# A fused Macaron block on one core: the third norm's rows turned by memory and VectorE instead of TensorE

## The reference, cut to what matters

```python
x = L0_attn_x                                   # (4, 1024, 1024) float32
x = x + 0.5 * ffn(layernorm(x))                 # first norm
x = x + attn(layernorm(x))                      # second norm
x = x + 0.5 * ffn(layernorm(x))                 # third norm

def ffn(input):      # same weights both times
    x = input.reshape(-1, 1024)
    hits = softmax(x @ centroids.T / 0.1) > 0.01          # 64 clusters
    query_sel = any(hits, axis=1)                         # per token
    row_sel = any(hits, axis=0)[assignments]              # per output column
    return where(query_sel[:, None] & row_sel[None, :], x @ weight.T + bias, 0)

def attn(x):         # per token: 32 heads as a 32 x 32 softmax over the head dimension
    q, k, v = x @ Wq + bq, x @ Wk + bk, x @ Wv + bv       # k and v: 8 heads, each repeated 4 times
    scores = einsum('bsdh,bseh->bsde', q, k) / sqrt(32)
    return einsum('bsde,bseh->bsdh', softmax(scores), v)
```

## Time and profile before

| | us |
|---|---|
| median of 3 runs | 1257.59 |
| lowest, highest | 1253.80, 1264.04 |
| profiled execution: span from first to last instruction | 1253.4 |
| TensorE busy | 1224.9 |
| VectorE busy | 841.3 |
| ScalarE busy | 411.3 |
| GpSimd busy | 419.6 |

### The profile page before, as it was taken

The page is one execution under the profiler, slowest core; times in us unless marked ns, Lnnn a source line. Parts: engine busy times, 40 slices in busy tenths (PEclk is TensorE's granted clock), DMA queues, the critical chain, the costliest instruction groups (busy, mean ns, idle before and its releaser), DMA issues.

```text
span 1253.4 us, 21699 instructions
## 1 busy us (share of the span) xinstructions
PE 1224.9 (98%) x8552; PEld 1052.8 (84%) x8552; DVE 841.3 (67%) x1207; ACT 411.3 (33%) x590; POOL 419.6 (33%) x551
## 2 busy tenths in 40 slices
PE   6999999999998899999999999999999999999998
PEld 5778888888887788888888888888888888887886
DVE  5644355345452378878788787887878865279887
ACT  4313222322210134443444444444444443212120
POOL 1225544543423634323333333333332200040322
PEclk8999999999998999999999999999999999999999
DMA  7376776776663345555555555455555554116785
GB/s 260 101 210 184 231 199 201 198 223 176 168 179 117 110 124 155 156 135 163 156 139 157 141 158 162 133 160 139 152 160 133 148 142 162 67 51 236 275 302 193
DMA packets 318693, 208.53 MB, mean 166 GB/s; under 512 B 258304, under 2 KB 281344, under 8 KB 318592
## 3 DMA queue, kind: packets, MB, share of 16 engines
q1 hardware_dynamic: 303712, 187.74, 52.0%
q10 hardware_dynamic: 14880, 19.40, 4.5%
HBM read 118.49 MB, written 88.60 MB: 165 GB/s over the span
## 4 chain that ended last, share of the span: by engine, by line
PE 90%; DVE 3%; DMA 2%; ACT 1%; issue 1%; SPq 1%; POOL 1%; POOLq 0%; DVEq 0%; ACTq 0%
PE ps_b L269 13%; PE ps_b L271 13%; PE ps_b L270 13%; PE ps_a L269 11%; PE ps_a L271 10%; PE ps_a L270 10%; PE ps_t L276 6%; PE ps_s L1348 5%; PE ps_s L283 2%; PE ps_s L285 2%; PE ps_s L1398 2%; PE ps_s L290 1%; DMA y_scratch<-xa 1%; SPq L398 1%; DMA ya_tok<-y_scratch 1%
## 5 line engine op out<-in xcount | busy, mean ns | idle before, releaser
L269 PE MATMUL ps_a<-w_hi,odd_hi 128*128 128x512 f32 x464 | 186.4, 402 | 0.0
L271 PE MATMUL ps_a<-w_hi,odd_lo 128*128 128x512 f32 x464 | 182.1, 392 | 0.0
L270 PE MATMUL ps_a<-w_lo,odd_hi 128*128 128x512 f32 x464 | 181.6, 391 | 0.0
L269 PE MATMUL ps_b<-proj_hi,y_hi 128*128 128x256 f32 (+1 forms) x512 | 177.7, 347 | 0.0
L271 PE MATMUL ps_b<-proj_hi,y_lo 128*128 128x256 f32 (+1 forms) x512 | 172.7, 337 | 0.0
L270 PE MATMUL ps_b<-proj_lo,y_hi 128*128 128x256 f32 (+1 forms) x512 | 172.0, 336 | 0.0
L303 POOL TENSOR_TENSOR var_eps<-moments,eps 128x1 f32<-128x1 f32 x96 | 18.4, 191 | 406.2 <-DVE moments L299 406.2
L661 POOL TENSOR_TENSOR x_ring<-x_ring,f_tmp 128x1024 f32<-128x1024 f32 x32 | 77.0, 2405 | 163.6 <-DVE probs L1112 135.4
L962 DVE TENSOR_TENSOR f_out<-ps_b,bias_a 128x512 f32<-128x512 f32 x30 | 20.7, 689 | 147.9 <-PE ps_b L271 147.9
L607 POOL TENSOR_SCALAR f_out<-f_out,token_on 128x1024 f32<-128x1024 f32 x30 | 85.6, 2854 | 88.3 <-DVE f_out L962 88.0
L271 PEld LDWEIGHTS ps_b<-proj_hi,y_lo 128*128 128x128 f32 x512 | 97.1, 190 | 10.8
(11 more groups left out here) (188 smaller groups left out, 2731.5 us busy)
## 6 DMA issues: line engine op xcount, KB each, us to landing
xa<-in_L_attn_x SPq DMA_DIRECT2D x32, 512.0 KB, 5.2
f_tmp<-f_scratch SPq DMA_DIRECT2D x32, 512.0 KB, 4.4
x_ring<-in_L_attn_x SPq DMA_DIRECT2D x32, 512.0 KB, 3.3
f_scratch<-f_out SPq DMA_DIRECT2D x30, 512.0 KB, 4.0
x_scratch<-x_ring SPq DMA_DIRECT2D x30, 512.0 KB, 3.3
y_scratch<-xa SPq DMA_DIRECT2D x28, 512.0 KB, 3.7
ya_tok<-y_scratch SPq DMA_DIRECT2D x112, 128.0 KB, 3.2
late<-x_scratch SPq DMA_DIRECT2D x22, 512.0 KB, 6.9
```

Source lines behind the costliest of these rows:

```text
L269: pe.matmul(acc, hi[:, k, :], w_h[:, k, cols], start=(k == 0), stop=False)
L270: pe.matmul(acc, hi[:, k, :], w_l[:, k, cols], start=False, stop=False)
L271: last = pe.matmul(acc, lo[:, k, :], w_h[:, k, cols], start=False, stop=(k == KB - 1))
```

## The change

The third norm's tiles 0 to 29 are no longer turned by TensorE. ScalarE writes the norm into a buffer of its own (`y3_tok`) in an order of blocks; SP stores it to memory (`y3_d`) and loads it back (`y3_turn`) with the 32-row blocks side by side; VectorE transposes the 32 x 32 blocks; ScalarE copies the high part from SBUF, writing every fourth column, and **Pool** subtracts for the low part. The kept tiles 1 and 3 and the late tiles 5 to 29 are loaded from `y3_d` again, so that their norms are not computed twice. Tiles 30 and 31 stay with TensorE (`transpose_end`, `high_end`, `low_end`).

To make room for the round trip the order changes: `high_third` and the low part come one iteration after the norm, third products go from `i-5` to `i-6` with two of them in the last iteration, and pair logits and pair softmax go one iteration back.

```diff
+    y3_d = nc.dram_tensor("y3_scratch", (NT - 2, T4, P, EMB // T4), F32, kind="Internal").ap()
+            y3_tok, y3_turn = sb2("y3_tok", [P, EMB]), sb2("y3_turn", [P, EMB])
-        late_y = [probs, f_tmp]
+        late_y = [y3_turn, y3_tok, probs, f_tmp]
+        def turned(tile):
+            return tile[:, :].rearrange("p (b k i) -> p b k i", b=T4, k=KB)
+        def by_block(tile):
+            return tile.rearrange("p k (i b) -> p b k i", b=T4)
 # SP
+                def store_y3(t):
+                    sp.wait_ge(y3, t + 1)
+                    sp.dma_start(y3_d[t].rearrange("a p f -> p a f"), y3_tok[:, :]).then_inc(y3_stored, 16)
+                def load_y3(t):
+                    sp.wait_ge(y3_stored, 16 * (t + 1))
+                    wait(sp, lo3, t)
+                    sp.dma_start(y3_turn[:, :], y3_d[t].rearrange(TURNED, b=T4)).then_inc(y3_in, 16)
+                def load_again(e):
+                    ...
+                    wait(sp, loe, e)
+                    sp.dma_start(f_tmp[:, :], y3_d[2 * e + 1].rearrange(TURNED, b=T4)).then_inc(ye_in, 16)
+                def load_late_y(v):
+                    ...
+                    wait(sp, lol, v - 4)
+                    sp.dma_start(late_y[n][:, :], y3_d[LATE[v]].rearrange(TURNED, b=T4)).then_inc(yl_in[n], 16)
                     if 3 <= i < NT + 1:
                         load_x(i + 1)
+                    if 0 <= i - 4 < NT - 2:
+                        store_y3(i - 4)
 ...                     # behind the q, k loads and the v store of iteration i
+                    if 0 <= i - 4 < NT - 2:
+                        load_y3(i - 4)
 # Pool
+                def low_third(t):
+                    hi, lo = third_set(t)
+                    pool.wait_ge(hi3, t + 1)
+                    pool.tensor_tensor(by_block(lo), turned(y3_turn),
+                                       by_block(hi.bitcast(F32)), ALU.subtract).then_inc(lo3, 1)
                     if i + 1 < NT:
                         mask_first(i + 1)
+                    if 0 <= i - 5 < NT - 2:
+                        low_third(i - 5)
+                    if i - 1 >= NT:
+                        low_again(i - 1 - NT)
+                    if i + 1 < NT:
                         add_first(i + 1)
+                for v in range(1, NL):
+                    for k in READY_OF[v - 1]:
+                        mask_ready(k)
+                    if 3 <= v + 1 < NL:
+                        low_late(v + 1)
 # ScalarE
+                def norm_third(t):
+                    act.wait_ge(norm3, t + 1)
+                    wait(act, y3_stored, 16 * t)
+                    normed(act, y3_tok[:, :].rearrange("p (a k j) -> p k a j", a=T4, k=KB), ...
+                def high_third(t):
+                    act.wait_ge(turn3, t + 1)
+                    ...
+                        if t % 2 == 0:
+                            act.wait_ge(ffn3, t)
+                    act.copy(by_block(third_set(t)[0]), turned(y3_turn)
+                             ).then_inc(hi3, 1)
+                    if 0 <= i - 6 < len(HALVES):
+                        store_third(i - 6)
                     if i == NT + 2:
-                        norm_third(NT - 2, i)
-                    if 0 <= i - 5 < len(HALVES):
                         store_third(i - 5)
+                        norm_end(NT - 2)
                     if 0 <= i - 4 < NT - 2:
-                        norm_third(i - 4, i)
+                        norm_third(i - 4)
+                    if 0 <= i - 5 < NT - 2:
+                        high_third(i - 5)
 # VectorE
+                def turn_third(t):
+                    dve.wait_ge(y3_in, 16 * (t + 1))
+                    dve.transpose(y3_turn[:, :], y3_turn[:, :]).then_inc(turn3, 1)
+                    if 0 <= i - 5 < NT - 2:      # ahead of row_max
+                        turn_third(i - 5)
-                    if 0 <= i - 4 < NT - 1:      # ahead of the transpose of probs
-                        low_third(i - 4)
 # TensorE
-                    if 0 <= i - 5 < len(HALVES):
+                    if 0 <= i - 6 < len(HALVES):
+                        product_third(i - 6)
+                    if i == NT + 2:
                         product_third(i - 5)
-                    if 0 <= i - 4 < NT - 1:
-                        transpose_third(i - 4, i)
-                    if NT <= i < NT + 2:
-                        transpose_again(i - NT)
-                    if v + 1 < NL:
-                        transpose_late(v + 1)
```

More of the change, by code:

```diff
@@ L186, in half, with wait_third @@
             return slice(h * HALF, (h + 1) * HALF)
+        def wait_third(eng, t):
+            if t < NT - 2:
+                eng.wait_ge(lo3, t + 1)
+            else:
+                eng.wait_ge(lo3_end, t - NT + 3)
         def wait(eng, semaphore, value):
@@ L561, in _ @@
                 sp.wait_ge(y3, NT - 2)
+                for v in range(1, 5):
+                    load_late_y(v)
                 load_late(4)
@@ L662, in add_first, with low_again, low_late @@
                                        ALU.add).then_inc(x1, 1)
+                def low_third(t):
[3 more added lines that the diff above has]
+                                       by_block(hi.bitcast(F32)), ALU.subtract).then_inc(lo3, 1)
+                def low_again(e):
+                    pool.wait_ge(hie, e + 1)
+                    pool.tensor_tensor(by_block(y2_lo[:, :, :]), turned(f_tmp), by_block(y2_hi[:, :, :].bitcast(F32)),
+                                       ALU.subtract).then_inc(loe, 1)
+                def low_late(v):
+                    hi, lo = late_set(v)
+                    pool.wait_ge(hil, v)
+                    pool.tensor_tensor(by_block(lo), turned(late_y[(v - 1) % 4]), by_block(hi.bitcast(F32)),
+                                       ALU.subtract).then_inc(lol, 1)
                 mask_first(0)
@@ L790, in high_again @@
                     act.wait_ge(te, e + 1)
[L791 to L797, removed]
+                    if e == 0:
+                        act.wait_ge(proj_v, NT)
+                    else:
+                        act.wait_ge(ffnk, 2)
+                    act.copy(by_block(y2_hi[:, :, :]), turned(f_tmp)).then_inc(hie, 1)
                 def keep_third(m):
@@ L829, in high_late @@
                 def high_late(v):
                     act.wait_ge(tl, v)
-                    act.copy(late_set(v)[0], ps_t[:, :, :]).then_inc(hil, 1)
-                def norm_third(t, i):
-                    act.wait_ge(norm3, t + 1)
-                    act.wait_ge(t2, min(i, NT))
-                    act.wait_ge(scores, min(i - 1, NT))
-                    wait(act, t3, t)
+                    if v == 1:
+                        act.wait_ge(ffnk, len(KEPT_HALVES))
+                        act.wait_ge(pair_done, 2 * NP)
@@ new lines, in high_third @@
+                def high_third(t):
+                    act.wait_ge(turn3, t + 1)
+                    if t < 2:
+                        act.wait_ge(pair_done, NP)
+                        for h in range(2):
+                            act.wait_ge(ffn1[h], NT - 1 + t)
+                    else:
+                        act.wait_ge(pair_done, NP + t // 2)
+                        if t % 2 == 0:
+                            act.wait_ge(ffn3, t)
+                    act.copy(by_block(third_set(t)[0]), turned(y3_turn)
+                             ).then_inc(hi3, 1)
@@ L838, in norm_third, with norm_end, high_end @@
+                def norm_end(t):
+                    act.wait_ge(norm3, t + 1)
+                    act.wait_ge(t2, NT)
+                    act.wait_ge(scores, NT)
+                    wait(act, t3, t - NT + 2)
                     normed(act, y_tok[:, :], x_ring[t % RING][:, :], 2, t).then_inc(y3, 1)
-                def high_third(t):
-                    act.wait_ge(t3, t + 1)
+                def high_end(t):
+                    act.wait_ge(t3, t - NT + 3)
+                    act.wait_ge(ffn3, len(HALVES))
+                    act.wait_ge(pair_done, 2 * NP - 1)
@@ L1040, in _, with turn_again, turn_late @@
                 scores_v = ps_s[:, :].rearrange(GROUPS, e=D)
[L1042 to L1050 removed]
+                def turn_again(e):
+                    dve.wait_ge(ye_in, 16 * (e + 1))
+                    dve.transpose(f_tmp[:, :], f_tmp[:, :]).then_inc(te, 1)
+                def turn_late(v):
+                    y = late_y[(v - 1) % 4]
+                    dve.wait_ge(yl_in[(v - 1) % 4], 16 * ((v - 1) // 4 + 2))
+                    dve.transpose(y[:, :], y[:, :]).then_inc(tl, 1)
                 def add_heads(t):
@@ L1072, in _ @@
                     if i - 1 >= NT:
-                        low_again(i - 1 - NT)
-                    if i >= 6 and i % 2 == 0:
-                        pair_soft_in(dve, NP + (i - 6) // 2)
+                        turn_again(i - 1 - NT)
+                    if i >= 7 and i % 2 == 1:
+                        pair_soft_in(dve, NP + (i - 7) // 2)
```

(4 more changed lines are left out.)

148 lines of the change are left out of this document (71 added, 77 removed).

## The result

The changed kernel takes 1319.2 us (median of 4 runs, 1314.2 to 1327.4) beside 1257.3 us of the kernel before on the same chip: ratio 1.0499, 95% interval 1.0458 to 1.0540. The forecast was 1273, the range 1242 to 1294. The sign was right, the size was not: 62 us slower instead of 15. (The profiled spans, 1253.4 and 1319.1 us, lie 66 apart, since the one before is the fastest of its runs.)

What follows compares the result with a forecast made beforehand. TensorE, busy 98% of the span, was taken as the bound. Up to the mask -2.2 us and the last stage +17 gave +15 (14.8) on 1257.6: forecast 1273 us, range 1242 to 1294.

Steps and rivals of the forecast that it cites:

- The query chain: Attention stage: query-key projection to ready queries takes 9.5 us against TensorE's 10.1, so 0.6 us stay; cost 0.
- +14: Attention stage: cost if the y3 load sat in front of q, 1.1 us per pair of iterations, 13 pairs.
- the attention stage slips as well: Rival, chance 0.16: y3's round trip lands late or q is held, +14, and slow Pool ops; 1287 to 1296.
- The clock, 4.5: Up to the mask: slower TensorE clock behind each of three idle times, 1.5 us a time, 4.5 us.
- Iteration 5, 4.9: Attention stage: iteration 5 has no third product, so TensorE's 4.6 us against the chain's 9.5 leaves 4.9 us idle.
- The kept tiles, 8.2 + 9.95 = 18.15: Iterations 33 and 34: TensorE idles for Pool's low_again behind low_third, 8.2 us before the first kept product, then 9.95.
- The sizes the trace lacked: Assumed times of strided operations: Pool's subtraction 2.9 us (2.40 to 3.5), ScalarE's strided write 1.3 us (1.05 to 2.65).
- The last stage, +17: Behind the mask: Pool's low parts block VectorE's two-SBUF-input instructions; VectorE needs 13.2 us per period and becomes the bound, +17 us.
- the 9.6 that the transposes were to give: Last stage: the 11 transpose sets removed behind the second mask would save 9.6 us if nothing was lost.
- VectorE ahead of row_max and SP's queue, cost 0: Attention stage: VectorE's turn (1.23 us) before row_max and SP's later loads and stores still come in time; cost 0 each.

Runs made afterwards that it cites:

- after, store on ScalarE: Changed kernel, with ScalarE issuing the new 512 KB store right behind the norm, the load staying in its place on SP: 1306.8 us, ratio 1.0387.
- after, load ahead only: Changed kernel, with SP issuing the y3_turn load right behind the query-key store, ahead of the query loads; store stays on SP: 1330.0 us, ratio 1.0576.
- run 8: Changed kernel with store on ScalarE, load behind query-key store, low_again ahead of low_third on Pool, last stage as before the change: 1262.7 us, ratio 1.0049.
- run 9: Changed kernel, attention-stage store and load cut from 512 KB to 64 KB each, third norm's data not right: 1287.6 us, ratio 1.0224.
- run 4: Changed kernel, Pool's low part of the late tiles cut to 8 of 1024 columns: 1296.7 us, ratio 1.0326.
- run 7: Changed kernel, the load going to a buffer nobody reads and VectorE turning probs instead, third norm's data wrong: 1318.4 us, ratio 1.0491.
- run 1: Changed kernel, ScalarE issuing the y3 store behind its norm and SP the y3 load right behind the query-key store: 1294.7 us, ratio 1.0309.
- Runs 2 and 10: Kernel before plus idle 512 KB store and load per tile: at the changed kernel's places, 1277.9 us; store on ScalarE, load behind query-key store, 1264.7 us.

## Why the prediction was wrong

*The query chain, "cost 0": this step failed.* It took the landings of the kernel before as they were, 9.5 us for the chain against 10.1 of TensorE's work, "0.6 us stay". It checked that the new load stands behind the query's load. But "the y3 store behind load_x" puts the new 512 KB store ahead of the query-key store and of the query's load, and that place was given no cost. SP's issues before the change, then after it:

```profile
711.16 0.37 SPq L517 DMA_DIRECT2D qkv_scratch<-qkv_tok  x1
714.15 0.57 SPq L521 DMA_DIRECT2D q_head<-qkv_scratch  x1
```
```profile
698.08 0.43 SPq L499 DMA_DIRECT2D y_scratch<-y_tok  x1
700.54 0.37 SPq L565 DMA_DIRECT2D qkv_scratch<-qkv_tok  x1
704.70 0.57 SPq L569 DMA_DIRECT2D q_head<-qkv_scratch  x1
```

From the issue of the query-key store to that of the query's load, which waits for it, it is now 4.33 us (mean of 18), where it was 3.01, and the chain is 10.88 us, 1.23 more: twice the slack. The order of the runs follows the chain. The last column is free of what the executions differ by ahead of the first new transfer:

| kernel | query chain, us | mean iteration, us | first to last row_max, us |
|---|---|---|---|
| before | 9.65 | 19.43 | 597.3 |
| before, traffic | 10.99 | 20.16 | 620.1 |
| before, traffic placed | 9.74 | 19.65 | 607.5 |
| after | 10.88 | 19.99 | 614.8 |
| after, store on ScalarE | 10.18 | 19.66 | 603.5 |
| after, load ahead only | 11.08 | 20.42 | 627.4 |
| after, both moved | 9.81 | 19.25 | 594.2 |
| after, 64 KB | 9.76 | 18.77 | 582.2 |

Within the rows that have the transposes and within those that don't, the longer chain goes with the longer iteration (run 8, 10.09 and 19.09, is the clear exception). It isn't all: from both moved to 64 KB the chain loses 0.05 and the iteration 0.48 us, so the bytes cost something at another place too, which stays open. The price of "+14" for a transfer ahead of q had the right form, 1.1 us in each of 13 pairs of iterations; measured are 12 waits of 1.9 us, 22.9 in all outside iteration 5. But it was taken as a case that doesn't arise. The rival "the attention stage slips as well" (0.16) named it ("or q is held"), though its 1287 to 1296 were too low as well.

*The clock, 4.5: mis-sized, 19.0 measured.* It was priced for three idle times of the forecast's length. There were 21 waits, and the granted clock is 0.82, 0.80 and 0.80 in the three short windows above, 0.98 over the whole middle, where it was 1.00. The mechanism was right; it cost 0.9 us per wait on average, and the count was wrong, since the waits for the queries were missing from it.

*Iteration 5, 4.9: 7.8 measured,* and 9.4 in run 8. The query chain that this wait ends on took 11.97 us from the read, where the prediction's rows have 9.3 (710.44 to 719.77): 2.6 of the 2.9 us of difference. In run 8 it took 13.16. Before the change the chain at this place took 9.19. It is 12.11 in run 9 too, so at this one place the 64 KB transfers didn't shorten it; why it is so long there stays open.

*The kept tiles, 8.2 + 9.95 = 18.15: right,* 9.3 + 10.3 = 19.6 measured. The chain of waits of the changed kernel ahead of the first and of the second:

```profile
1052.51 1.26 DVE y_turn L1162
1053.78 2.01 ACT odd_hi L933
1055.86 2.87 POOL odd_lo L725
1058.73 2.82 POOL y_lo L730
1061.59 0.79 PE ps_b L285
...
1087.45 0.39 ACT f_out L899
...
1089.67 1.98 ACT odd_hi L933
1091.72 2.86 POOL odd_lo L725
1094.57 2.82 POOL y_lo L730
1097.43 0.80 PE ps_b L285
```

In the first, the load (issued at 1047.08, 5.40 us) and the turn stand ahead of the high part, not store_third and the norm. In the second the norm is in its place (it is most of the 1.11 us of "issue"). So the second term was right in its links, the first in its size by luck.

*The sizes the trace lacked.* All instructions of the two lines in the changed kernel:

```profile
L725 POOL TENSOR_TENSOR odd_lo<-y_turn,odd_hi x30: 2856/2963/3002, 496.3 to 1091.7; 128x1024 fp32r<-128x1024 f32 x30
...
L933 ACT CAST odd_hi<-y_turn x30: 1972/2042/2070, 494.1 to 1089.7; 128x1024 fp32r<-128x1024 f32 x30
```

Pool 2.96 us for the 2.9 taken; ScalarE 2.04 for 1.3, inside its bounds (1.05 to 2.65) but not "near the row of the same shape". The Trainium skill (GPSIMD Engine Reference, Performance pitfalls for Q7 kernels) has 50% more for such a read; the trace does not agree, as the measured 2.96 is 23% over the 2.40 of the unit-step add, and the measurement decides.

*The last stage, +17: right,* +20.4 measured, by the named cause. The timeline of VectorE in the changed kernel, and then Pool's of the same time:

```profile
1201.59 1.28 DVE L1265 SCALAR_TENSOR_TENSOR late<-k_diag,token_on,late 128x1024 f32<-128x1024 f32 x1
1202.90 3.75 DVE L1267 SCALAR_TENSOR_TENSOR late<-late,token_on 128x1024 f32<-128x1024 f32 x1
1206.58 0.74 DVE L1247 SCALAR_TENSOR_TENSOR v_diag<-ps_b,token_on,mask 128x512 f32<-128x512 f32 x1
1207.35 1.85 DVE L1254 TENSOR_TENSOR v_pad<-v_pad,v_diag 128x512 f32<-128x512 f32 x1
```
```profile
1202.69 2.88 POOL L736 TENSOR_TENSOR odd_lo<-y_tok,odd_hi 128x1024 fp32r<-128x1024 f32 x1 [8.53 <-ACT odd_hi L915]
1205.54 3.12 POOL L777 TENSOR_TENSOR late<-late,mask 128x1024 f32<-128x1024 f32 x1
```

L1267, 1.28 us alone, takes 3.75 and ends 1.1 us behind Pool's operation, which began 0.2 before it: so it got almost nowhere until Pool was through. L1247, which reads PSUM, keeps 0.74 beside Pool's next one. This is what the Trainium skill (SBUF — State Buffer, SBUF: two separate sides) states as an exclusive lock, and the trace agrees. With the low parts cut (run 4) the stage takes 145.5 us, so their price is 23.5; even then it is only 3 us shorter than before the change, of the 9.6 that the transposes were to give.

*VectorE ahead of row_max and SP's queue, cost 0: right for the first but for a little* (run 7: without its wait, no gain in time; TensorE's waits for probs, 2.9 us in the changed kernel, are 0.6 there), *right in the sum for the second* (run 9: with the same issues and waits and an eighth of the bytes, no loss).

## What to carry to other kernels

Work taken off the full engine pays only as far as the next chain behind it has slack, and that slack must be read with the new traffic in it: two transfers per tile that nobody waits for cost 21 us when one of them was issued right ahead of a store on the critical chain, and 6 us when it was issued earlier and by another engine. When a load is moved ahead in a queue, move the store that it waits for ahead first. Idle time of TensorE counts more than once, by the clock: here 54 us of waits came with 19 us of slower products.

## What was not expected of the hardware

From the issue of the query-key store (256 KB) to that of the load that waits for it, it took 3.0 us in a stage with a DMA share of 0.54, and 4.3 us with a mean share of 0.71 when 512 KB had been issued just ahead of it; at 0.73, with those bytes issued some 6 us ahead and by ScalarE (run 1), 3.4. Runs 2 and 10, which differ in the places of the transfers only, have 4.5 and 3.2 us at shares of 0.70 and 0.71. So the mean share didn't tell the delay; what had been issued just ahead did. And ScalarE's write with a step of four elements takes 2.04 us where the unit-step one takes 1.05. What stays open is whether the hole in iteration 5 could be filled by another order of the products: that wasn't tried.
